# One step table for all engines: two attention layers over four images, with projections placed inside attention and one-tile score banks

## Chip, cores and metric

One core of one Trainium2 chip. The metric is the device time of one execution in microseconds (us); the median of three runs is used. Times within one profiled execution are read from its trace, where the span is the time from the first to the last instruction. Engine names of the profile: PE (TensorE matmuls), PEld (its weight loads), DVE (VectorE), ACT (ScalarE), POOL (GpSimd), SP (SyncE).

## The reference

x is (4, 256, 64, 64) in float32, that is four images of 256 channels by 4096 positions.

```python
# layer 0, per image; x is 256 x 4096
q, k, v = Wq @ x + bq, Wk @ x + bk, Wv @ x + bv      # 32, 32, 256 channels
attn = softmax(q.T @ k, over the rows i)             # 4096 x 4096
x = gamma * (v @ attn) + x
# layer 1, per image
theta = theta_w @ x + theta_b                        # 32 channels, 4096 positions
phi   = maxpool2(phi_w @ x + phi_b)                  # 32 channels, 1024 positions
g     = maxpool2(g_w @ x + g_b)                      # 128 channels, 1024 positions
out   = g @ softmax(theta.T @ phi).T                 # 128 x 4096
x = gamma * (out_w @ out + out_b) + x
```

## The kernel before

**Tiles.** Positions whose attention is computed come in 8 chunks of 512 (`NCH`, `CH`). The keys come in tiles of 128: 32 tiles in layer 0, 8 in layer 1 (`KT`). Scores of a tile are 128 keys x 512 positions. Values and keys are kept in two parts, a high part in fp32r and a low part, the difference; probabilities are split in the same way. So each tile costs one scores matmul, and for each of the 2 (layer 0) or 1 (layer 1) blocks of 128 output channels three matmuls: high by high, high by low (L927, `prob_h`), low by high (L927, `prob_l`).

**Stages.** For each image in turn: `project0` for 8 chunks (keys, queries and values of layer 0, from x rounded by ScalarE, L446, and its rest made by GpSimd, L373), attention of layer 0, `project1` for 8 chunks (g with a max pool, keys and queries of layer 1), prologue maxima, attention of layer 1. x of an image lies whole in SBUF in `x_sb` and is rewritten in place by layer 0 and by layer 1; it is stored and the next image's chunk is loaded into its place by SyncE (L334, L326).

**Softmax.** The greatest score of a position is needed ahead of its chunk. Matmuls `ST` (L832) make the scores transposed, 128 positions x 512 keys, into an auxiliary bank, and VectorE reduces each to a maximum (L605). From the maxima of a chunk VectorE makes `nm_wide` (`finish_max`, L611 to L616), four matmuls `M` (L840) turn it into rows which VectorE writes into `queries` (L623), and the scores matmul then subtracts the maximum by itself. ST and M of chunk n + 1 (layer 0) or n + 2 (layer 1) run within chunk n.

**Step of attention.** A step holds two tiles. TensorE makes the scores of the next step (L914, into one of two `s_ps` of two banks each), then the low matmuls of the last step, then the high ones of this step; the places of ST, M, D1, D2 and Z between them are written out in `PLANS`. ScalarE takes exp twice over 128 x 1024 (L487 into `prob`, L491 into `prob_h`). GpSimd subtracts (L382, `prob_l`). VectorE adds both tiles of `prob` into the PSUM bank `acc` (L704).

**End of a chunk.** ScalarE copies `o_ps[0]` (L502) and `acc` (L509), VectorE copies `o_ps[1]` (L749). D1 (L946) sums over partitions, VectorE takes the reciprocal (L715), D2 (L951) spreads it, VectorE multiplies (L723 in layer 0, L720 in layer 1). In layer 0 VectorE also adds the bias and x (L732). In layer 1 Z (L956) is the output convolution, ScalarE drains it (L517), GpSimd adds x (L389). The fp32 matmuls D1, D2 and Z are two instructions each.

**Order.** Each engine works through its own queue in order; semaphores alone tie the queues together. PSUM has 8 banks: four for `s_ps`, two for `o_ps`, `acc` and `aux`. In the projection stages the four banks of `s_ps` hold the projections, so scores cannot run then.

## Time and profile before

| what | value |
|---|---|
| median of 3 runs | 2927.06 us (2925.76 to 2927.38) |
| the profiled execution | 2925.82 us, of which 2924.0 us span |
| mean granted TensorE clock | 0.97 of full |
| PE busy | 2771.6 us (95%), 12260 matmuls |
| PEld busy | 2156.4 us (74%) |
| DVE busy | 2119.7 us (72%), 3369 instructions |
| ACT busy | 1585.5 us (54%), 1827 instructions |
| POOL busy | 1763.6 us (60%), 776 instructions |
| DMA | 36.41 MB, mean 12 GB/s |

Matmuls are pipelined: the duration of one in the profile, about 0.4 us for 512 columns, is about twice the distance between the starts of two in a row. So TensorE's busy share says only that something was in its pipeline; for the work one counts matmuls and takes the distance of starts.

### The profile page before, as it was taken

How to read it: one execution, taken by the hardware profiler on the slowest of the kernel's cores; microseconds unless marked ns; L12 is line 12 of the kernel's file. 1: busy time of each engine (PE TensorE's matmuls, PEld its weight loads, DVE VectorE, ACT ScalarE, POOL GpSimd, SP SyncE). 2: the span in 40 equal slices, each digit the busy share in tenths (PEclk: the TensorE clock that was granted, in tenths of full speed). 3: DMA queues.
4: the chain of work that ended last, by engine and by line, in shares of the span. 5: the costliest groups of instructions: out<-in, count | busy, mean ns of one | idle time of the engine just before them, and what ended most of it. 6: DMA issues, size and time to landing. Idle time of an engine off the chain costs nothing.

```text
span 2924.0 us, 33409 instructions
## 1 busy us (share of the span) xinstructions
PE 2771.6 (95%) x12260; PEld 2156.4 (74%) x12260; DVE 2119.7 (72%) x3369; ACT 1585.5 (54%) x1827; POOL 1763.6 (60%) x776
## 2 busy tenths in 40 slices
PE   7999999989999999998999999998899999999888
PEld 6877777756787777865677777776567777778665
DVE  7777777676777777767677777776757777777685
ACT  5545545657555555565665555556566545555655
POOL 3665665658466666665746666666574566666557
PEclk9999999989899999998989999999899999999988
DMA  2000000002000000000200000000020000000001
GB/s 68 1 0 1 1 1 1 1 15 72 30 1 1 1 1 1 1 0 22 73 22 1 1 1 1 1 1 1 27 73 17 1 1 1 1 1 1 1 15 44
DMA packets 18131, 36.41 MB, mean 12 GB/s; under 512 B 1200, under 2 KB 1328, under 8 KB 17968
## 3 DMA queue, kind: packets, MB, share of 16 engines
q1 hardware_dynamic: 17408, 33.56, 3.5%
q8 instruction: 97, 1.59, 0.2%
q10 hardware_dynamic: 560, 0.73, 0.1%
q14 instruction: 66, 0.54, 0.1%
HBM read 17.50 MB, written 16.78 MB: 12 GB/s over the span
## 4 chain that ended last, share of the span: by engine, by line
PE 80%; DVE 13%; ACT 3%; issue 3%; DMA 0%; POOL 0%; ACTq 0%; POOLq 0%
PE o_ps L927 52%; PE s_ps L914 9%; PE aux L832 9%; DVE mx L605 5%; PE aux L951 2%; DVE vl L628 2%; DVE acc L704 2%; ACT queries L457 1%; DVE queries L629 1%; PE o_ps L946 1%; PE aux L956 1%; PE aux L840 1%; PE o_ps L956 1%; PE o_ps L832 1%; PE aux L946 1%
## 5 line engine op out<-in xcount | busy, mean ns | idle before, releaser
L382 POOL TENSOR_TENSOR prob_l<-prob,prob_h 128x1024 fp32r<-128x1024 f32 x640 | 1530.5, 2392 | 985.0 <-ACT prob_h L491 983.1
L487 ACT ACTIVATE prob<-s_ps 128x1024 f32<-128x1024 f32 x640 | 657.5, 1027 | 1101.8 <-PE s_ps L914 1078.0
L605 DVE TENSOR_REDUCE mx<-aux 128x1 f32<-128x512 f32 x1088 | 750.6, 690 | 382.5 <-PE aux L832 358.3
L927 PE MATMUL o_ps<-prob_h,vh 128*128 128x512 f32 x2304 | 938.2, 407 | 10.3 <-ACT prob_h L491 3.4
L927 PE MATMUL o_ps<-prob_h,vl 128*128 128x512 f32 x2304 | 913.4, 396 | 0.0
L704 DVE TENSOR_TENSOR acc<-prob,acc 128x512 f32<-128x512 f32 x1216 | 836.5, 688 | 73.4 <-ACT prob L487 60.3
L927 PE MATMUL o_ps<-prob_l,vh 128*128 128x512 f32 x2304 | 685.2, 397 | 1.5 <-POOL prob_l L382 1.5
L491 ACT ACTIVATE prob_h<-s_ps 128x1024 fp32r<-128x1024 f32 x640 | 654.2, 1022 | 0.0
L927 PEld LDWEIGHTS o_ps<-prob_h,vh 128*128 128x128 f32 x2304 | 438.7, 190 | 127.1 <-ACT osb L502 25.0
L927 PEld LDWEIGHTS o_ps<-prob_l,vh 128*128 128x128 f32 x2304 | 435.7, 190 | 102.6 <-POOL prob_l L382 6.0
L927 PEld LDWEIGHTS o_ps<-prob_h,vl 128*128 128x128 f32 x2304 | 438.8, 190 | 94.3 <-issue 6.7
L832 PE MATMUL aux<-keys,queries 96*128 96x512 f32 x1088 | 458.3, 421 | 41.7 <-DVE mx L605 36.3
L914 PE MATMUL s_ps<-queries,keys 128*128 128x512 f32 x1280 | 413.4, 405 | 3.3 <-issue 3.3
L832 PEld LDWEIGHTS aux<-keys,queries 96*128 96x128 f32 x1088 | 208.4, 192 | 138.2 <-DVE mx L605 63.0
L914 PEld LDWEIGHTS s_ps<-queries,keys 128*128 128x128 f32 x1280 | 242.6, 194 | 61.2 <-DVE queries L623 6.7
L373 POOL TENSOR_TENSOR xl<-x_sb,xh 128x1024 fp32r<-128x1024 f32 x64 | 152.3, 2381 | 147.4 <-ACT xh L446 147.4
L605 DVE TENSOR_REDUCE mx<-o_ps 128x1 f32<-128x512 f32 x192 | 131.3, 684 | 6.4 <-PE o_ps L832 4.8
L832 PE MATMUL o_ps<-keys,queries 96*128 96x512 f32 x192 | 90.0, 469 | 16.9 <-DVE mx L605 14.8
L389 POOL TENSOR_TENSOR x_sb<-zc,x_sb 128x512 f32<-128x512 f32 x64 | 81.2, 1273 | 24.1 <-ACT zc L517 24.1
L732 DVE SCALAR_TENSOR_TENSOR x_sb<-osb,gbv,x_sb 128x512 f32<-128x512 f32 x64 | 89.8, 1408 | 0.1
L457 ACT ACTIVATE queries<-s_ps,cols 32x512 fp32r<-32x512 f32 x128 | 87.0, 679 | 3.2
L502 ACT ACTIVATE osb<-o_ps 128x512 f32<-128x512 f32 x64 | 38.2, 597 | 92.2 <-PE o_ps L927 92.2
(72 smaller groups left out, 1822.5 us busy)
## 6 DMA issues: line engine op xcount, KB each, us to landing
x_sb<-x SPq DMA_DIRECT2D x32, 512.0 KB, 3.7
y<-x_sb SPq DMA_DIRECT2D x32, 512.0 KB, 2.8
prob<-w_in ACTq DMA_DIRECT2D x1, 576.0 KB, 5.2
wo<-w_out ACTq DMA_DIRECT2D x1, 128.0 KB, 6.0
cols<-columns ACTq DMA_DIRECT2D x1, 4.5 KB, 6.1
```

Source lines behind the costliest of these rows:

```text
L373: nc.gpsimd.tensor_tensor(out=xl[par][:, :, :], in0=x_sb[:, :, chunk(c)], in1=xh[par][:, :, :].bitcast(f32), op=ALU.subtract).then_inc(xl_ ...
L382: nc.gpsimd.tensor_tensor(out=prob_l[i][:, :, :], in0=prob[i], in1=prob_h[i][:, :, :].bitcast(f32), op=ALU.subtract).then_inc(pl_ready, 1)
L389: nc.gpsimd.tensor_tensor(out=x_sb[:, ct, chunk(n - 1)], in0=zc[:, ct, :], in1=x_sb[:, ct, chunk(n - 1)], op=ALU.add).then_inc(y_ready, 1)
L457: nc.scalar.activation(dst, src, ACT.Identity, bias=cols[rows, COL_KQ[l]:COL_KQ[l] + 1]).then_inc(hi_ready, 1)
L487: nc.scalar.activation(prob[i], s_ps[i][:, :, :], ACT.Exp).then_inc(p_ready, 1)
L491: nc.scalar.activation(prob_h[i][:, :, :], s_ps[i][:, :, :], ACT.Exp).then_inc(ph_ready, 1)
L605: nc.vector.tensor_reduce(out=mx[:, sub, c], in_=aux_bank[bank][:, :], axis=AX.X, op=ALU.max).then_inc(aux_free[bank] if done is None else ...
L704: nc.vector.tensor_tensor(out=acc[:, :], in0=prob[i][:, t, :], in1=acc[:, :], op=ALU.add).then_inc(acc_done, 1)
L732: ins = nc.vector.scalar_tensor_tensor(out=x_sb[:, ct, chunk(n - 1)], in0=osb[:, ct, :], scalar=gbv[:, ct:ct + 1], in1=x_sb[:, ct, chunk(n ...
L832: mm(aux_bank[bank][:, :], queries[0:R3, ds(n * CH + sub * P, P)], keys[0:R3, chunk(c)], start=True, stop=True).then_inc(aux_full[bank], 1)
L914: last = mm(s_ps[i][:, t, :], keys[:, kt * P:(kt + 1) * P], queries[:, chunk(n)], start=True, stop=True)
L927: ins = mm(o_ps[ct][:, :], value, (prob_l if low else prob_h)[s % 2][:, t, :], start=not low and k % 2 == 0 and kt == 0, stop=low and kt = ...
```

## The change

All work is laid out once, in `make_plan`, as jobs at steps of one table of 1280 tiles (32 or 8 per chunk). Every engine walks the same table and takes of each job what is its own part. A tile is one step; scores have three banks of one tile (`SRING`), probabilities four slots of one tile (`RING`), scores are made two tiles ahead (`AHEAD`), splits and sums one. The three banks for jobs are X0, X1 and Y, which is `o_ps[1]` and free in layer 1 only.

Within layer 0's attention of chunk n run the jobs for chunk n - 1 of layer 1: XB (ScalarE adds the bias to x), N (GpSimd adds x), X (rounding and rest), G1, K1, K1K, K1L, T1, T1L (projection of layer 1, VectorE's and ScalarE's parts of it). Within layer 1's attention run the projections K0, V0 (drained by ScalarE, low parts K0L, V0L by VectorE) of chunks 4 to 7 of the next image in chunks 1 to 4, and the maxima of its chunk 0. Between layer 0 and layer 1 of an image stands one list (`before[tile_no(1, b, 0)]`), with the last projection of layer 1 and the first four of the next image; layer 1's scores start behind it (`gated`). Layer 0 of the second to fourth image has no such list. The first image has a list of its own (`before[0]`).

x no longer stays in SBUF. `xp` has two slots for projections of layer 0, the first two loads issued by SyncE and the others by ScalarE. `xa` has four slots: SyncE loads a chunk of x again for layer 0's residual, stores the result to a DRAM tensor `spill`, loads it back for layer 1's residual and stores y. The final part of layer 0's residual moves from VectorE (L732) to ScalarE (bias) and GpSimd (add).

The diff, cut to its core:

```diff
-DIST = (1, 2)
-        x_sb = sb("x_sb", [P, CT, N])
-        s_ps = [pb(f"s_ps{i}", [P, 2, CH]) for i in range(2)]
-        aux_bank = (aux, o_ps[1])
...
+RING = 4
+SRING = 3
+AHEAD = 2
+QSLOTS = 12
+ASLOTS, PSLOTS = 4, 2
+X0, X1, Y = range(3)
...
+def gated(l, b):
+    return l == 1 or b == 0
+def begin_step(h, ahead):
+    l, b, _, _ = tile_at(h)
+    return max(h - ahead, tile_no(l, b, 0) if gated(l, b) else 0)
+def begun_at(g, ahead):
+    return [h for h in range(g, min(g + ahead + 1, TILES)) if begin_step(h, ahead) == g]
...
+    def project0(b, c, banks):
+        k, v0, v1 = banks
+        return [on(Job("K0", 0, b, c, 0), k), on(Job("V0", 0, b, c, 0), v0), on(Job("V0", 0, b, c, 1), v1)]
+    def put(g, place, job):
+        during.setdefault(g, []).append(Entry(place, job))
...
+    lists = []
+    for c in range(NCH):
+        k, v0, v1 = project0(0, c, (X1, Y, X0 if c == 0 else Y))
+        if c == 0:
+            lists += [first[0], first[1], k, Job("K0L", 0, 0, 0, 0), v0, Job("V0L", 0, 0, 0, 0),
+                      v1, Job("V0L", 0, 0, 0, 1)]
+        else:
+            if c + 1 < NCH:
+                lists.append(first[c + 1])
+            st = [maxima(0, 0, 0, c - 1, s, X0) for s in range(SUBS)]
+            lists += [st[0], k, st[1], v0, Job("K0L", 0, 0, c, 0), st[2], Job("V0L", 0, 0, c, 0), v1, st[3],
+                      Job("V0L", 0, 0, c, 1)]
+    lists += [maxima(0, 0, 0, NCH - 1, s, X0 if s % 2 == 0 else X1) for s in range(SUBS)]
+    lists.append(on(Job("M", 0, 0, 0, 0), X0))
+    before[0] = lists
...
+            if prev is not None:
+                put(g, 1, on(Job("D1", *prev, 0), X1))
+                put(g + 2, 1, on(Job("D2", *prev, 0), X1))
+                if prev[0] == 0:
+                    c = prev[2]
+                    put(g + 1, 1, Job("XB", *prev, 0))
+                    put(g + 3, 1, Job("N", *prev, 0))
+                    put(g + 7, 1, Job("X", 1, b, c, 0))
+                    put(g + 10, 1, on(Job("G1", 1, b, c, 0), X1))
+                    put(g + 13, 1, on(Job("K1", 1, b, c, 0), X1))
+                    put(g + 14, 1, Job("K1K", 1, b, c, 0))
+                    put(g + 15, 1, Job("K1L", 1, b, c, 0))
+                    put(g + 17, 1, on(Job("T1", 1, b, c, 0), X1))
+                    put(g + 18, 1, Job("T1L", 1, b, c, 0))
+                else:
+                    for k in range(CT):
+                        put(g + 4 + 2 * k, 1, on(Job("Z", *prev, k), X1))
+                        put(g + 5 + 2 * k, 1, Job("ZA", *prev, k))
+            if n + 1 < NCH:
...
+                steps = [(i, X0) for i in range(27)] + [(i, X1) for i in range(20, 25)]
+                steps.sort()
+                for i, (t, at) in enumerate(steps):
+                    put(g + t, 1 if at == X1 else 3, maxima(0, b, n + 1, i // SUBS, i % SUBS, at))
+                put(g + 28, 1, on(Job("M", 0, b, n + 1, 0), X1))
+            else:
+                for i in range(SUBS * (NCH - 1)):
+                    put(g + i, 3, maxima(1, b, i // SUBS, 0, i % SUBS, X0))
+                if more:
+                    put(g + 21, 1, Job("X", 0, b + 1, 0, 0))
+                    put(g + 27, 1, Job("X", 0, b + 1, 1, 0))
...
+            before[tile_no(1, b, 0)] = (
+                chain1 + [k0] + chain2[:2] + [low("K0L", 0, 0), v00, low("V0L", 0, 0), v01, low("V0L", 0, 1)]
+                + chain2[2:] + [k1_, low("K0L", 1, 0), v10, low("V0L", 1, 0), v11, low("V0L", 1, 1),
+                                Job("X", 0, b + 1, 2, 0)]
+                + chain3 + [Job("X", 0, b + 1, 3, 0)]
+                + [st[0][0], k2, st[0][1], low("K0L", 2, 0), st[0][2], v20, st[0][3], low("V0L", 2, 0), v21, m0,
+                   low("V0L", 2, 1)]
+                + [k3, st[1][0], v30, low("K0L", 3, 0), st[1][1], low("V0L", 3, 0), v31, st[1][2], low("V0L", 3, 1), st[1][3],
+                   Job("X", 0, b + 1, 4, 0)])
...
+            if more:
+                for s, (t, at) in enumerate(((0, X1), (0, Y), (2, Y), (3, Y)) if n < NCH - 1 else
+                                            ((0, X1), (0, Y), (1, X1), (1, Y))):
+                    put(g + t, 3, maxima(0, b + 1, 0, n, s, at))
+                c = n + 3
+                if n >= 1 and c < NCH:
+                    k, v0, v1 = project0(b + 1, c, (X1, X1, X1))
+                    put(g + 1, 1, k)
+                    put(g + 3, 1, Job("K0L", 0, b + 1, c, 0))
+                    put(g + 4, 1, v0)
+                    put(g + 5, 1, Job("V0L", 0, b + 1, c, 0))
+                    put(g + 6, 1, v1)
+                    put(g + 7, 1, Job("V0L", 0, b + 1, c, 1))
+                    if c + 1 < NCH:
+                        put(g + 7, 1, Job("X", 0, b + 1, c + 1, 0))
...
+        xa = [sb(f"xa{i}", [P, CT, CH]) for i in range(ASLOTS)]
+        xp = [sb(f"xp{i}", [P, CT, CH]) for i in range(PSLOTS)]
+        keys = (sb("keys0", [P, KT[0] * P], f32r), sb("keys1", [P, KT[1] * P], f32r))
+        queries = sb("queries", [P, QSLOTS, CH], f32r)
...
+        s_ps = [pb(f"s_ps{i}") for i in range(SRING)]
+        o_ps = [pb(f"o_ps{i}") for i in range(2)]
+        acc = pb("acc")
+        aux = (pb("aux0"), pb("aux1"), o_ps[1])
...
+            for k in range(B * 2 * NCH):
+                l, b, n = k // NCH % 2, k // (2 * NCH), k % NCH
+                store_a(l, b, n)
+                nxt = k + ASLOTS
+                if nxt < B * 2 * NCH:
+                    slot, turn = a_slot(l, b, n)
+                    sp.wait_ge(xa_out[slot], 16 * (turn + 1))
+                    if l == 0:
+                        sp.wait_ge(xl_ready, ROUND[Job("X", 1, b, n, 0)] + 1)
+                    load_a(nxt // NCH % 2, nxt // (2 * NCH), nxt % NCH)
...
+            def entry(job):
+                name, l, b, c, k = job
+                if name == "X":
+                    r = ROUND[job]
+                    src = xa[a_slot(0, b, c)[0]] if l else xp[image0(b, c) % PSLOTS]
+                    pool.wait_ge(xh_ready, r + 1)
+                    nc.gpsimd.tensor_tensor(out=xl[r % 2][:, :, :], in0=src[:, :, :],
+                                            in1=xh[r % 2][:, :, :].bitcast(f32),
+                                            op=ALU.subtract).then_inc(xl_ready, 1)
+                elif name == "N":
+                    slot, _ = a_slot(0, b, c)
+                    pool.wait_ge(xb_ready, CT * image0(b, c) + CT)
+                    for ct in range(CT):
+                        if ct == 0:
+                            pool.wait_ge(normed, image0(b, c) + 1)
+                        else:
+                            wait_free(pool, Job("D2", 0, b, c, 0))
+                        nc.gpsimd.tensor_tensor(out=xa[slot][:, ct, :], in0=osb[:, ct, :], in1=xa[slot][:, ct, :],
+                                                op=ALU.add).then_inc(x1_ready, 1)
...
+            for g in range(TILES):
+                for job in BEFORE.get(g, ()):
+                    entry(job)
+                for h in begun_at(g, 1):
+                    split_prob(h)
+                for e in DURING.get(g, ()):
+                    entry(e.job)
...
+            def exps(h):
+                i, s = h % RING, h % SRING
+                act.wait_ge(s_full, h + 1)
+                wait(act, pl_ready, h - RING + 1)
+                wait(act, acc_done, h - RING + 1)
+                nc.scalar.activation(prob[:, i, :], s_ps[s][:, :], ACT.Exp).then_inc(p_ready, 1)
+                wait(act, av_h, h - RING + 1)
+                nc.scalar.activation(prob_h[:, i, :], s_ps[s][:, :], ACT.Exp).then_inc(ph_ready, 1)
...
+                elif name == "V0":
+                    wait_full(act, job)
+                    at = c * SUBS + 2 * k
+                    nc.scalar.activation(vh[0][:, at:at + 2, :], bank[:, :].rearrange("p (t m) -> p t m", t=2),
+                                         ACT.Copy).then_inc(high_ready, 1)
+                    p = image0(b, c) + PSLOTS
+                    if k == 1 and p < B * NCH:
+                        load_p(p)
...
+            for g in range(TILES):
+                l, b, n, t = tile_at(g)
+                if t == 0 and g:
+                    copy_o(*chunk_before(l, b, n))
+                for job in BEFORE.get(g, ()):
+                    entry(job)
+                for h in begun_at(g, AHEAD):
+                    exps(h)
+                if t == KT[l] - 1:
+                    copy_acc(l, b, n)
+                for e in DURING.get(g, ()):
+                    entry(e.job)
...
+            for g in range(TILES):
+                l, b, n, t = tile_at(g)
+                prev = chunk_before(l, b, n)
+                if t == 0 and prev is not None and prev[0] == 0:
+                    copy_o(*prev[1:])
+                for job in BEFORE.get(g, ()):
+                    entry(job)
+                fresh = t == KT[l] - 1
+                if not fresh:
+                    for h in begun_at(g, 1):
+                        add_prob(h)
+                for e in DURING.get(g, ()):
+                    entry(e.job)
+                if fresh:
+                    for h in begun_at(g, 1):
+                        add_prob(h)
...
+            def scores(h):
+                l, b, n, t = tile_at(h)
+                if t == 0:
+                    wait_free(pe, Job("M", l, b, n, 0))
+                wait(pe, ph_ready, h - SRING + 1)
+                mm(s_ps[h % SRING][:, :], keys[l][:, t * P:(t + 1) * P], queries[:, q_slot(l, b, n), :],
+                   start=True, stop=True).then_inc(s_full, 1)
...
+                if g:
+                    av_low(g - 1)
+                for job in BEFORE.get(g, ()):
+                    entry(job)
+                for h in begun_at(g, AHEAD):
+                    scores(h)
+                entries_at(1)
+                av_high(g, 0)
+                entries_at(2)
+                if VT[l] > 1:
+                    av_high(g, 1)
+                entries_at(3)
```

## Rows read from the trace of the kernel before

**Rows 1.** The page's slices: granted clock in 40 equal parts of the span, tenths of full.
```profile
PEclk9999999989899999998989999999899999999988
```

**Rows 2.** Windows view: stretch, its length, then busy us and instructions (x) by engine, clock, DMA.
```profile
0.00:66.50 66.50, 50.67 (x285) 41.19 (x285) 51.11 (x79) 37.77 (x54) 20.40 (x17) 0.95 0.23 75
...
792.40:1283.00 490.60, 486.16 (x2146) 392.81 (x2147) 356.42 (x549) 254.68 (x270) 306.80 (x129) 0.99 0.00 1
1283.00:1341.80 58.80, 43.66 (x157) 26.68 (x156) 42.56 (x70) 26.54 (x43) 20.75 (x9) 0.84 0.00 0
1341.80:1454.20 112.40, 106.11 (x459) 76.13 (x458) 83.57 (x150) 75.66 (x90) 87.46 (x43) 0.96 0.18 57
1454.20:1519.00 64.80, 56.95 (x309) 43.92 (x307) 45.84 (x72) 38.90 (x56) 25.49 (x14) 0.89 0.10 33
913.30:976.20 62.90, 62.25 (x277) 50.10 (x276) 47.71 (x75) 32.05 (x35) 38.33 (x17) 1.00 0.00 1
1379.40:1394.70 15.30, 14.43 (x66) 10.11 (x65) 12.02 (x23) 10.06 (x12) 12.06 (x7) 1.00 0.22 70
```

**Rows 3.** Timeline at a chunk boundary of layer 0: start, length (us), engine, line.
```profile
1167.63 1.07 PE L927 MATMUL o_ps<-prob_l,vh 128*128 128x512 f32 x4
1168.54 0.61 PE L914 MATMUL s_ps<-queries,keys 128*128 128x512 f32 x2
...
1168.73 0.69 DVE L749 COPY osb<-o_ps 128x512 f32<-128x512 f32 x1 [2.21 <-PE o_ps L927]
...
1169.53 0.47 PE L927 MATMUL o_ps<-prob_h,vh 128*128 128x512 f32 x1
```

**Rows 4.** Timeline of TensorE near the end: a Z and a D2.
```profile
2908.81 1.02 PE L956 MATMUL o_ps<-osb,wo 128*128 128x512 f32 x2
...
2912.72 1.13 PE L951 MATMUL aux<-ident,rsum 128*128 128x128 f32 x8 [0.37 <-DVE rsum L715]
```

**Rows 5.** Windows view within the stage between layers 0 and 1.
```profile
1293.00:1323.00 30.00, 21.50 (x84) 12.45 (x82) 23.38 (x36) 20.46 (x35) 14.19 (x6) 1.00 0.00 1
1323.00:1341.80 18.80, 13.44 (x28) 7.41 (x29) 13.57 (x26) 2.55 (x4) 2.34 (x1) 0.51 0.00 0
```

**Rows 6.** Groups by line and shape: busy us, mean ns, then idle before and releaser.
```profile
L382 POOL TENSOR_TENSOR prob_l<-prob,prob_h 128x1024 fp32r<-128x1024 f32 x640 | 1530.5, 2392 | 985.0 <-ACT prob_h L491 983.1
L605 DVE TENSOR_REDUCE mx<-aux 128x1 f32<-128x512 f32 x1088 | 750.6, 690 | 382.5 <-PE aux L832 358.3
L487 ACT ACTIVATE prob<-s_ps 128x1024 f32<-128x1024 f32 x640 | 657.5, 1027 | 1101.8 <-PE s_ps L914 1078.0 <-DVE acc L704 23.4 <-POOL prob_l L382 0.4
L832 PE MATMUL aux<-keys,queries 96*128 96x512 f32 x1088 | 458.3, 421 | 41.7 <-DVE mx L605 36.3 <-DVE queries L623 4.6
L457 ACT ACTIVATE queries<-s_ps,cols 32x512 fp32r<-32x512 f32 x128 | 87.0, 679 | 3.2
L389 POOL TENSOR_TENSOR x_sb<-zc,x_sb 128x512 f32<-128x512 f32 x64 | 81.2, 1273 | 24.1 <-ACT zc L517 24.1
L502 ACT ACTIVATE osb<-o_ps 128x512 f32<-128x512 f32 x64 | 38.2, 597 | 92.2 <-PE o_ps L927 92.2
```

**Rows 7.** Timeline of DVE and POOL in the projections of layer 1.
```profile
1291.37 0.34 DVE L629 SCALAR_TENSOR_TENSOR keys<-ppool,cols,keys 32x128 fp32r<-32x128 f32 x1 [0.47 <-ACT keys L457]
...
1294.27 2.37 POOL L373 TENSOR_TENSOR xl<-x_sb,xh 128x1024 fp32r<-128x1024 f32 x1 [5.78 <-ACT xh L446]
...
1295.63 1.15 DVE L629 SCALAR_TENSOR_TENSOR keys<-ppool,cols,keys 32x128 fp32r<-32x128 f32 x1 [0.47 <-ACT keys L457]
```

**Rows 8.** The chain that ended last, in order of time, in the first projections.
```profile
18.17 0.92 PE s_ps L848 x4
...
41.52 1.19 DVE mx L605 x2
...
47.03 1.19 DVE mx L605 x2
```

**Rows 9.** The page's DMA issues: KB each, median us from issue to landing.
```profile
x_sb<-x SPq DMA_DIRECT2D x32, 512.0 KB, 3.7
```

1136 lines of the change are left out of this document (461 added, 675 removed), and 4 rows, old and new, of the table PLANS.

## Prediction

> **What bounds the kernel now.** I read the page's slices first, then the busy time by stage, then single steps in order of time. The slices show the granted TensorE clock at 0.8 to 0.9 of full in a few places, which recur with the images [rows 1]. The stage table gives the period of an image (the second): 490.6 us attention of layer 0, 58.8 us of projections of layer 1 and its first maxima, 112.4 us attention of layer 1, 64.8 us of tail, projections of layer 0 and maxima, 726.6 us in all [rows 2]. TensorE is the bound where attention runs: 277 matmuls in the 62.9 us of one chunk of layer 0. Four matmuls of 512 columns start in 0.91 us, 0.228 us each [rows 3]. By the program 256 of them are long (32 scores, 192 for the output, 32 for maxima), 58.4 us, and 20 short (two sums steps, one for M), at 0.11 us each (eight issue within a 1.13 us row whose last 0.25 us is pipeline [rows 4]), 2.2 us. So 60.6 us is work and 2.3 us is stall. In layer 1 a chunk of 15.3 us holds 40 long matmuls (9.1 us), 20 short (2.2) and two output convolutions at 0.85 us each (the row of 1.02 us less its pipeline end [rows 4]): 13.0 us of work, 2.3 of stall [rows 2].
> The two stages between are bound by chains, not by TensorE: 157 and 309 matmuls in 58.8 and 64.8 us, and half the speed (0.51) in the last 19 us of the first [rows 2, 5]. The work of a whole image, counted by the same pitches, is about 650 us. The change goes for the other 75.
>
> **Attention of layer 0.** Work as before, and now the projection of one chunk of layer 1 in each of seven chunks: 12 long matmuls and a transposition, 12 x 0.228 + 0.25 = 3.0 us. It lies on TensorE, so it is paid in full: 63.6 us. Tiles of one bank: a step is 8 matmuls, 1.83 us. ScalarE had two exps of 1024 columns, 1.03 us each; a 512-wide copy is 0.60 [rows 6], so two exps are at most 1.2 and, if they overlap a little, 1.1 us per step: 60%. VectorE has an add and a maximum, 1.2 to 1.4 (0.69 one). GpSimd's difference is 2.39 us at 1024 and an add at 512 is 1.27 [rows 6]: 1.27 of 1.83. None is the bound. Waits per tile instead of per two tiles: 320 more on TensorE in an image. No row shows a wait's own cost. A chunk has some 80 now; its 2.3 us of stall, all put down to them, would be 0.03 each, 10 us an image. I take 0, as the long ones in a row keep 0.228, and leave the 10 us to the range.
> Stalls, by walking the queues from these durations. (a) GpSimd: at step 7 it has the split of x behind its split of tile 8. ScalarE rounds x only behind its exps of tile 9 (scores in at 0.9, 1.1, 1.0), so GpSimd stands until 3.1 us into the step, then works 2.38; the split of tile 9 ends at 6.7 us, and the low matmuls of tile 9 open step 10, at 5.5. Stall 1.2 us, once in a chunk. The two adds of the residual at step 3 (2.5 us, moved here from VectorE) end with 0.2 us to spare. (b) Chunk boundary: before, the high matmul starts 0.99 us after scores behind the last low one [rows 3]. Now the eight sums matmuls lie in front of that wait, which hides ScalarE's copy; but VectorE first adds tile 0 of the next chunk, which waits for the copy of acc, and only then copies o_ps (0.69 us [rows 3]). About 0.5 us of stall. (c) The single bank X0 for maxima: round trip 0.42 + 0.69 us of 1.83 [rows 6], so VectorE may be 0.6 us late; the two normalising multiplications and the low part of the keys go over that by 0.3 us in all. (d) Small gaps left, 1.0 us. Sum 3.0, a chunk 66.6 us. ScalarE's two added bias copies at step 1 find slack. SyncE's queue now writes every chunk of layer 0 out, reads it back and loads x a second time: four transfers where two were. A load lands 3.7 us after issue [rows 9], with three chunks of 15 us or more ahead of its use; cost 0, and 3.7 us a chunk if that lead were gone.
> The first chunk of an image has no projection but the last two convolutions of the image before: 60.6 + 1.7 + 1.7 = 64.0 (60.3 for the first image, which has neither). The last has 28 maxima instead of 32 and no row for M, but two more roundings of x with their stall: 63.6 - 1.4 + 3.0 + 2.4 = 67.6 (65.3 in the last image). Attention is 64.0 + 6 x 66.6 + 67.6 = 531.2 us (527.5 first, 528.9 last), 41 more than before.
> That low part of the keys took 0.34 us while GpSimd stood, and 1.15 us when a GpSimd subtraction of 2.37 us had begun before it, ending with it [rows 7]. It moves from a stage where GpSimd is busy 35% into attention, where it is 61% now and 75% after [rows 2]; between the two durations I take 0.85 us, which (c) contains. The Trainium skill, "SBUF — State Buffer" (section "SBUF: two separate sides"), says that a VectorE operation with two SBUF inputs and a GpSimd operation take one port pair exclusively, the later one waiting for the whole of the other. The rows agree. By it the wait can be all of a 1.27 us split each time, 0.8 more than I take; on the path, 28 x 0.8 = 22 us, 2938 us instead of my sum.
>
> **Between layer 0 and 1.** Layer 1's scores stay behind a gate, with one list ahead of it: the last projection of layer 1, four projections of the next image, eight maxima. Walked from the last low matmul: normalised at 4.9 us, x rounded behind three drains of ScalarE at 9.9, split at 12.4; TensorE meanwhile does three of the projections' halves; layer 1's conv ends at 17.8, VectorE's and ScalarE's drains of it at 21.9; eight maxima (each 1.2 us round trip on one bank), interleaved with two projections, whose drains VectorE takes in between, end at 41. TensorE works 25 of it. The nearest stretches: 84 matmuls in 30 us held the clock at 1.00; 28 in 18.8 us ran at 0.51 [rows 5]. At 0.228 that is 64% and, at most, 34% of the time; mine is 61%, near the first, so I take full clock: 39.5 to 54, taken 41.5 us. In the last image, without the next one's work, the chain alone is 29 us.
>
> **Attention of layer 1.** Chunks 1 to 4 carry a whole projection of the next image: 6 long and 24 half matmuls, 4.3 us. ScalarE then has 16 x 0.5 exps, copies, drains (0.68 for each query part [rows 6]), a rounding and the issue of a load: about 15 us; VectorE 14, GpSimd 15.1 (8 x 1.27 + 2 x 1.27 + 2.38), TensorE 17.3. All four are close, queues are in order and scores are only two tiles ahead: stall 2.5, 19.8 us. The others: 15.1, with 12.8 for the first and 14.1 for the last two. Sum 12.8 + 79.2 + 15.1 + 28.2 = 135.3 us against 112.4. In the last image, with no foreign work and four maxima less a chunk, 109 (11.5 + 5 x 14.2 + 2 x 13.2). There is no gate into the next layer 0: of the 64.8 us nothing stays.
> A period is then 531.2 + 41.5 + 135.3 = 708.0 us, 18.6 less than 726.6.
>
> **The first image** pays. Before, its loads are all in flight early and a chunk costs 5.5 us, VectorE's time (41.52 to 47.03) [rows 8]; its first output matmul starts at 66.5 us [rows 2]. After, only two slots hold x; the load of chunk c + 2 is issued by ScalarE behind its last drain of chunk c, and the rounding of chunk c + 2 is the first thing in ScalarE's list of chunk c + 1. So the list of c + 1 opens with a landing of 3.7 us [rows 9], then rounding 1.05, the three query and key drains 2.0, VectorE's low parts and a maximum and the low value part, together 2.8; and since both value halves use bank Y, the second half's 12 matmuls (1.4 + 0.3) and its drain 0.6 follow. Sum 12.1 us at full clock, 13.5 at half; TensorE is busy 40% there, between the two stretches of [rows 5], so 12.8. The first chunk is done at 18.0, as now, when the second's matmuls start [rows 8]. Six such: 18.0 + 76.8 = 94.8, then the last chunk, four maxima and the first exps, 17.3: first output at 112 us, 45 later. Its cover would be an earlier issue; there is none.
>
> **Sum.** 112 + 527.5 + 41.5 + 135.3 = 816.3; two images of 708.0: 2232.3; the last 528.9 + 29 + 109 + 15 of tail (now the Z at 2908.81 [rows 4] lies 15.2 ahead of the end) = 2914.2 us of span. The profiled run had 1.8 us around its span and lay 1.2 below the median of 2927.06. Forecast 2916.0 us, 0.4% less.
>
> **Rivals.** (1) Faster, 2853: slack absorbs the queue stalls, layer 0 chunks take 65.0 (28 x 1.6) and the twelve loaded chunks of layer 1 18.3 (18 us). For: VectorE loses the residual adds, and a late TensorE gives every other engine time. Against: one bank for maxima, one tile of lead for splits. (2) Slower, 2972: GpSimd's queue in layer 0. The adds at step 3 end with only 0.2 us to spare; if each entry of GpSimd comes some 0.5 to 1 us later, both stall, a chunk takes 68.6, 28 x 2.0 = 56 us. It decides from 0.4 us per chunk on (11 us over 28). For: the walk puts one entry past due. Against: a late TensorE gives the others time back. (3) Slower, 2961: the change doesn't take away what it says. The gate before layer 1 stays, and with gaps in it the clock falls: 54 instead of 41.5 us thrice, and 8 more at the front, 45 us. For: 0.51 in the same place now. Against: more matmuls per us than there.
>
> **Chances.** Forecast (2895 to 2935) 0.40, of which 0.27 lies below, 0.08 within, 0.05 above; rival 1 0.25; rival 2 0.22; rival 3 0.13. A measurement of this kernel can tell about 0.2% (6 us) from no change. Faster 0.27 + 0.25 = 0.52, same 0.08, slower 0.40. The range goes to both sides, 2840 to 2975 us.
>
> **What would show it.** Chunks of layer 0 at 66.6 us with a TensorE wait for the split of tile 9; first output matmul at 112 us; from the last output matmul of layer 0 to the first of layer 1 41 us at clock 1.00; loaded chunks of layer 1 at 20 us; no gap into the next image. It is wrong if the first output comes before 90, or a layer 0 chunk is under 65 or over 68 us.

## The result, and the profile after

The changed kernel takes 2949.15 us (median of six runs, 2935.74 to 2955.05) beside 2927.22 us for the kernel before on the same chip: a ratio of 1.007, 95% interval 1.0047 to 1.0093. It is 0.7% slower; the forecast was 2916.0 us, 0.4% faster. The profiled execution took 2952.56 us, of which 2950.8 us is span, 26.8 us more than before's 2924.0.

The page of the changed kernel: totals, the clock in slices, the two groups that changed most.

```profile
span 2950.8 us, 39091 instructions
...
PE 2757.0 (93%) x12260; PEld 2180.1 (74%) x12260; DVE 2008.1 (68%) x3303; ACT 1750.7 (59%) x3171; POOL 1949.9 (66%) x1480
...
PEclk7799999998999999999899999999999999999989
...
DMA packets 44280, 87.10 MB, mean 30 GB/s; under 512 B 2736, under 2 KB 2864, under 8 KB 44080
...
L427 POOL TENSOR_TENSOR prob_l<-prob,prob_h 128x512 fp32r<-128x512 f32 x1280 | 1639.7, 1289 | 751.6 <-ACT prob_h L490 744.2
L487 ACT ACTIVATE prob<-s_ps 128x512 f32<-128x512 f32 x1280 | 768.5, 600 | 974.2 <-PE s_ps L765 973.5
```

TensorE issues the same 12260 matmuls. Its busy time fell by 15 us and the span rose by 27, so this column does not tell the story. Against [rows 1] the slices changed place: the first two stand at 0.7 (0.9 before), where the first image now spends 50 us more, while the dips between the layers are shallower. In tiles of half the size GpSimd's splits cost 7% more (1530.5 us in [rows 6]) and ScalarE's first exps 17% more (657.5 us there).

The windows view, stretch by stretch, answers to [rows 2]. Columns: stretch, length, busy us (instructions) of PE, PEld, DVE, ACT, POOL, granted clock, DMA share, GB/s.

```profile
0.00:115.70 115.70, 69.60 (x284) 54.62 (x284) 53.12 (x76) 36.64 (x54) 20.16 (x17) 0.75 0.22 70
444.20:510.60 66.40, 64.77 (x290) 52.47 (x290) 47.24 (x78) 39.52 (x73) 45.89 (x36) 1.00 0.05 17
641.20:684.70 43.50, 32.78 (x171) 26.18 (x170) 23.90 (x41) 22.03 (x34) 11.98 (x7) 0.86 0.24 73
684.70:702.30 17.60, 16.58 (x56) 11.52 (x57) 13.89 (x25) 10.95 (x22) 13.17 (x11) 0.78 0.01 1
702.30:722.80 20.50, 18.77 (x96) 13.94 (x95) 15.39 (x28) 14.58 (x26) 11.87 (x10) 1.00 0.14 48
722.80:745.80 23.00, 21.79 (x94) 15.97 (x94) 15.11 (x27) 15.20 (x27) 15.02 (x12) 0.85 0.21 69
745.80:769.10 23.30, 21.66 (x95) 16.03 (x95) 15.16 (x27) 15.26 (x27) 15.10 (x12) 0.85 0.20 68
792.10:807.40 15.30, 14.16 (x66) 10.16 (x65) 12.39 (x23) 10.92 (x21) 11.87 (x10) 1.00 0.16 53
```

These are the time to the first output matmul, one chunk of layer 0, the stage between layers 0 and 1, and chunks 0, 1, 2, 3 and 5 of layer 1 of the first image. Compare the fifth row with the next two: the same jobs in 20.5 us at full clock and in 23.0 and 23.3 at 0.85. By the program the chunks hold the same matmuls.

The ledger of the three images that project a next one, first output matmul to first output matmul. The stage between the layers is counted from the last tile's high matmuls (641.2 in the first image), 0.9 us ahead of the last low one, from which the forecast walked:

| us | forecast | image 1 | image 2 | image 3 |
|---|---|---|---|---|
| to the first output matmul | 112 | 115.7 | | |
| attention of layer 0 | 527.5, 531.2, 531.2 | 525.5 | 527.0 | 527.0 |
| between the layers | 41.5 | 43.5 | 43.8 | 42.2 |
| attention of layer 1 and into the next image | 135.3 | 151.3 | 150.8 | 149.4 |

The last image took 524.0 + 32.4 + 104.0 + 14.2 = 674.6 us, where 681.9 was forecast (528.9 + 29 + 109 + 15). A period is 721.6 us (image 2), 5.0 less than the 726.6 before; 18.6 less was forecast. The first image is 43.6 us later than before at the first output matmul of the second (836.0 against 792.4), image 2 gives back 5.0, the other two 11.8 together: 26.8.

### The profile page after: what moved, and what is told of

The parts are those of the page before. It is cut to its first block, busy times and chain, and to the rows that moved or that the text cites. A ratio compares the mean times of both kernels' runs of the same rounds, so it can differ in the third digit from the quotient of the medians.

```text
span 2950.8 us, 39091 instructions
## 1 busy us (share of the span) xinstructions
PE 2757.0 (93%) x12260; PEld 2180.1 (74%) x12260; DVE 2008.1 (68%) x3303; ACT 1750.7 (59%) x3171; POOL 1949.9 (66%) x1480
## 2 busy tenths in 40 slices
DMA packets 44280, 87.10 MB, mean 30 GB/s; under 512 B 2736, under 2 KB 2864, under 8 KB 44080
## 4 chain that ended last, share of the span: by engine, by line
PE 77%; issue 9%; DVE 5%; ACT 5%; POOL 4%; DMA 1%; POOLq 0%; ACTq 0%; DVEq 0%
PE o_ps L797 30%; PE o_ps L775 16%; PE s_ps L765 8%; PE aux L828 8%; POOL prob_l L427 3%; PE aux L808 3%; PE aux L841 2%; ACT prob_h L490 2%; DVE mx L650 2%; PE aux L837 2%; PE aux L845 1%; PE aux L812 1%; PE aux L862 1%; PE o_ps L828 1%; PE o_ps L862 1%
## 5 line engine op out<-in xcount | busy, mean ns | idle before, releaser
L427 POOL TENSOR_TENSOR prob_l<-prob,prob_h 128x512 fp32r<-128x512 f32 x1280 | 1639.7, 1289 | 751.6 <-ACT prob_h L490 744.2
L487 ACT ACTIVATE prob<-s_ps 128x512 f32<-128x512 f32 x1280 | 768.5, 600 | 974.2 <-PE s_ps L765 973.5
L775 PE MATMUL o_ps<-prob_l,vh 128*128 128x512 f32 x2304 | 756.0, 400 | 37.4 <-POOL prob_l L427 37.0
L490 ACT ACTIVATE prob_h<-s_ps 128x512 fp32r<-128x512 f32 x1280 | 762.1, 595 | 0.0
L765 PE MATMUL s_ps<-queries,keys 128*128 128x512 f32 x1280 | 509.2, 399 | 0.8 <-DVE queries L669 0.8
L436 POOL TENSOR_TENSOR xl<-xp,xh 128x1024 fp32r<-128x1024 f32 x32 | 76.0, 2378 | 167.4 <-ACT xh L529 167.4
L436 POOL TENSOR_TENSOR xl<-xa,xh 128x1024 fp32r<-128x1024 f32 x32 | 76.5, 2391 | 52.2 <-ACT xh L529 52.2
L447 POOL TENSOR_TENSOR xa<-osb,xa 128x512 f32<-128x512 f32 x64 | 82.1, 1305 | 20.2 <-DVE osb L682 20.2
L837 PEld LDWEIGHTS aux<-ones,psums 128*128 128x128 f32 x512 | 62.4, 191 | 44.0 <-issue 43.6
L512 ACT ACTIVATE queries<-aux,cols 32x512 fp32r<-32x512 f32 x116 | 78.9, 680 | 19.0 <-PE aux L812 17.9
```

The costliest lines, as they stand in the source:

```text
L427: nc.gpsimd.tensor_tensor(out=prob_l[:, i, :], in0=prob[:, i, :], in1=prob_h[:, i, :].bitcast(f32), op=ALU.subtract).then_inc(pl_ready, 1)
L436: nc.gpsimd.tensor_tensor(out=xl[r % 2][:, :, :], in0=src[:, :, :], in1=xh[r % 2][:, :, :].bitcast(f32), op=ALU.subtract).then_inc(xl_read ...
L487: nc.scalar.activation(prob[:, i, :], s_ps[s][:, :], ACT.Exp).then_inc(p_ready, 1)
L490: nc.scalar.activation(prob_h[:, i, :], s_ps[s][:, :], ACT.Exp).then_inc(ph_ready, 1)
L765: mm(s_ps[h % SRING][:, :], keys[l][:, t * P:(t + 1) * P], queries[:, q_slot(l, b, n), :], start=True, stop=True).then_inc(s_full, 1)
L775: last = mm(o_ps[ct][:, :], value(vh, l, t, ct), prob_l[:, h % RING, :], start=False, stop=t == KT[l] - 1)
```

## Experiments

Each kernel is the changed kernel with one edit, unless it says otherwise. Ratios are against the kernel before, run beside it; the changed kernel itself stands at 1.007. Four kernels (the fill, the earlier rounding, GpSimd's queue and the first try on the first image) ran on a chip where the kernel before takes 2923.36 us, and the last two beside 2923.15; that is 4 us less than the 2927.22 beside the changed kernel, so a difference of their medians holds 4 us of chip. Chunk times are distances of the first output matmuls of chunks in the profiled execution. Two theories were open for layer 1. A: the loaded chunks (those with a projection of the next image) lose the clock in small stalls, and that is the larger part of the miss. B: their queues alone take 23 us.

**Keep TensorE busy at the boundary.** Five matmuls whose results are overwritten unread, around the sums at the start of chunks 1 to 5 of layer 1 (three images), so at both ends of every loaded chunk:

```
 elif name == "D1":
+    if filled:                      # layer 1, chunks 0 to 4
+        for _ in range(3): mm(dst, wh, wh)
     pe.wait_ge(psums_ready, ...)
     ...                             # the eight sums matmuls
+    if filled:
+        last.then_inc(full[at], 1)
+        wait(pe, free[X1], ...)
+        for _ in range(2): mm(aux[X1], wh, wh)
```

> Only change: at the first step of chunks 1 to 5 of layer 1 (images 1 to 3) TensorE gets five matmuls of 512 columns more, into free banks, three ahead of the sums and two behind them, where it waits in the changed kernel (0.86 us for the copy of acc, 0.56 us for the copy of o_ps). Their results are overwritten, so the output is the same. Theory A (the loaded chunks of layer 1 take 23 instead of 19.8 us because the granted clock falls to half for 6.8 us of each, and it falls because TensorE stands around the chunk boundary): the clock keeps 1.00 in most of them, loaded chunks take 19.8 to 20.5 us, the whole about 2925 us although work was added. Rival B (the queues of the four engines cost the 23 us by themselves, the clock is only a by-product): chunks stay at 23 us or grow by up to 1 us, the whole 2950 to 2965 us.

Measured: 2930.22 us (2925.8 to 2934.93, ten runs), ratio 1.0022 (1.0012 to 1.0032). Windows view of this kernel, chunks 0, 2 and 3 of layer 1:

```profile
682.60:700.30 17.70, 15.86 (x61) 11.49 (x62) 14.37 (x26) 11.40 (x22) 13.87 (x11) 0.90 0.01 3
720.90:741.40 20.50, 19.52 (x101) 14.77 (x100) 15.06 (x27) 15.05 (x27) 14.93 (x12) 1.00 0.22 77
741.40:761.90 20.50, 19.51 (x100) 14.75 (x100) 15.06 (x27) 15.04 (x27) 14.93 (x12) 1.00 0.23 77
```

All twelve loaded chunks take 20.5 us, none at half clock: 22.6 us less than in the changed kernel. Work was added, and the kernel became 19 us faster (15 when each is set against the kernel before beside it). Theory A holds. The timeline of TensorE in the changed kernel shows how the clock is lost:

```profile
743.62 0.40 PE L765 MATMUL s_ps<-queries,keys 128*128 128x512 f32 x1
744.48 1.02 PE L837 MATMUL aux<-ones,psums 128*128 128x1 f32 x8 [0.47 <-ACT psums L509]
745.82 0.50 PE L797 MATMUL o_ps<-prob_h,vh 128*128 128x512 f32 x1 [0.32 <-ACT osb L501]
...
748.17 1.11 PE L833 MATMUL o_ps<-ident_r,nm_wide 128*128 128x128 f32 x4 [0.54 <-DVE mx L650]
749.08 0.68 PE L808 MATMUL aux<-xh,wh 128*96 128x512 f32 x1
749.56 0.63 PE L808 MATMUL aux<-xh,wl 128*96 128x512 f32 x1
749.99 0.63 PE L808 MATMUL aux<-xh,wh 128*96 128x512 f32 x1
```

The starts of single rows, less the 0.23 us that a matmul takes, give the gaps: the sums matmuls start 0.6 us late, behind ScalarE's copy; they are of one column each; and the next output matmul stands another 0.3 behind the profile's end of them. Both waits are gone in the kernel with the fill. The clock is granted at half from 747.2 to 754.0, and matmuls of 512 columns then start 0.43 us apart (749.56, 749.99), where they start 0.23 apart at full clock. 6.8 us at half would be 3.4 us of work lost; such a chunk lost 2.5 to 2.9. The waits do not bring the fall every time: the boundary into the first loaded chunk has the same one before its sums (0.48 us at 701.42), and that chunk keeps full clock.

**Round the next x earlier.** In loaded chunks the rounding of the next chunk of x at step 2 instead of 7, so that ScalarE doesn't stand before the boundary with it.

```
-  put(g + 7, 1, Job("X", 0, b + 1, c + 1, 0))
+  put(g + 2, 1, Job("X", 0, b + 1, c + 1, 0))
```

> Only change: in the loaded chunks of layer 1 the rounding of the next x and its rest (ScalarE 1.06 us, GpSimd 2.38 us) stand at step 2 instead of step 7, so ScalarE's copies at the chunk boundary are not behind the rounding. Theory A (TensorE's wait at the boundary lets the clock fall): the wait of 0.56 us behind the sums goes, 0.6 to 1.0 us a chunk at once, and if the clock then stays up in part of the chunks 2 to 4 us a chunk: whole 2915 to 2940 us. Rival B (queues alone): 11 chunks x 0.6 to 1.0 = 7 to 11 us, the clock unchanged, 2940 to 2945 us. Rival C (GpSimd's queue is the tight one in these chunks; its 2.38 us in step 2 make later splits late): no gain or a loss.

Measured: 2927.5 us (2924.7 to 2931.57), ratio 1.0012 (1.0002 to 1.0021). The loaded chunks stay at 20.5 us (the fourth 20.1), so the 0.6 to 1.0 us that were to come off at once did not; but 11 of 12 are at full clock (one takes 21.9). The whole lies 22 us below the changed kernel (18 against the kernel before beside it) with no work removed; the loaded chunks, 246.2 us instead of 268.6, put that down to the clock again.

**Leave the traffic out.** The spill transfers carry 32 of 512 columns; the rest of layer 1's residual isn't computed from the right x.

```
+  sp.dma_start(xa[slot][:, :, 0:32], source[:, ..., n * CH:n * CH + 32])
+  return
   sp.dma_start(xa[slot][:, :, :], source[:, ..., chunk(n)])
```

> The transfers to and from the spill tensor move 32 of 512 columns, so layer 1's residual is wrong in the rest; number, place and waits of the transfers stay. Rival under test: the added traffic (87 MB against 36) is what the change pays for. If so the whole falls by 20 us or more. Theory: the transfers are hidden by three chunks of lead and cost nothing: every stage keeps its length, loaded chunks 20.5 us where the clock stays and 23 where it falls, whole 2930 to 2955 us.

Measured: 2938.65 us (2936.01 to 2944.18, three runs), ratio 1.0044. Chunks of layer 0 take 66.4 us as before the edit, loaded chunks 20.5, 20.5, 20.5, 20.1 in the first image, 22.1, 23.1, 23.4, 21.6 in the second and 20.5, 20.5, 22.1, 22.6 in the third. The whole is 10 us lower, but its three runs lie within the range of the changed kernel's six, and no chunk at full clock became shorter than in the kernels with the traffic. So the spill's part of the added traffic (36.41 MB before, 87.10 after) costs nothing that shows; the second load of x was left in and is not tested. More telling: within one execution the same instructions take 20.5 us where the clock holds and 23 where it falls.

**Put the projections back into the list.** Chunks 4 to 7 of the next image are projected between the layers instead of within layer 1, the same instructions. The query ring has 12 slots, so these queries overwrite those of the first four chunks of layer 1, whose output is that of other queries.

```
+  for c in range(4, NCH):
+      before[tile_no(1, b, 0)] += [kc, K0L, va, V0L, X(c + 1), vb, V0L]
...
-  if n >= 1 and c < NCH:
+  if n >= 99:
```

> One part undone: chunks 4 to 7 of the next image's layer 0 projections stand at the end of the list between the layers instead of inside layer 1's attention; everything else, the maxima inside it too, as in the changed kernel. By my account a loaded chunk of layer 1 costs 20.5 us at full clock and 23 at half for 6.8 us, an unloaded one 15.2: 4 x (5.3 to 7.8) = 21 to 31 us less an image there. A projection in the list costs a chain of about 7 to 8 us (key and query drains 2.0, low parts 1.5, value parts, rounding 1.06 and rest 2.4): 28 to 32 us more. Theory: about the same whole, 2945 to 2965 us, with clock lost in the list instead. Rival (projections inside attention are the cheap place, TensorE alone pays 4.3 us): 3 x 4 x (7.5 - 4.3) = 38 us more, 2980 us and above.

Measured: 2956.64 us (2952.97 to 2960.98), ratio 1.0103. Windows view of this kernel, the list, and chunk 3 of layer 1:

```profile
639.00:711.20 72.20, 52.97 (x291) 42.81 (x290) 34.52 (x56) 37.71 (x57) 19.60 (x11) 0.91 0.22 67
757.50:775.60 18.10, 16.96 (x65) 12.73 (x66) 12.33 (x23) 10.85 (x21) 12.39 (x11) 0.81 0.17 59
```

The list takes 72.2 us instead of 43.5, 7.2 us for each projection moved there; layer 1 takes 123.5 instead of 151.3, 7.0 less for each. So a projection within layer 1 costs at its own chunk nearly what it costs outside, although TensorE's part of it is 6 long and 24 half matmuls, 4.3 us in the forecast. At full clock it is 5.2 (20.5 against 15.3). Without load a chunk can still lose the clock: 15.3 becomes 18.1 in three of twelve and 16.9 in a fourth.

**GpSimd's queue in layer 0.** The forecast's stall (a). GpSimd's part of X goes one step later, behind its split of tile 9.

```
   put(g + 7, 1, Job("X", 1, b, c, 0))
+  put(g + 8, 1, Job("XL", 1, b, c, 0))
...
+  if name == "X" and l == 1 and c < NCH - 1: return    # GpSimd
+  if name in ("X", "XL"): ...
```

> Only change: GpSimd's part of the rounding of layer 1's x in layer 0's attention stands one step later (step 8) than ScalarE's (step 7), so GpSimd no longer stands waiting for ScalarE ahead of the split of tile 9. Theory (one stall of 1.2 us a chunk at step 10, as forecast): chunks of layer 0 65.2 instead of 66.4 us, the whole 2914 to 2920 us less what the clock scatters (about 10 us). Rival (the stall only moves to the split of tile 10 or to the conv at step 10): chunks 66.0 to 66.4 us, whole unchanged.

Measured: 2900.72 us (2896.38 to 2908.48), ratio 0.9924 (0.9905 to 0.9943): faster than both kernels. Chunks of layer 0 take 65.1 us instead of 66.4, every one. The changed kernel's timeline of POOL at that place, then its waits over five chunks (total, times, longest), then the same view of this kernel over five chunks:

```profile
980.13 1.29 POOL L427 TENSOR_TENSOR prob_l<-prob,prob_h 128x512 fp32r<-128x512 f32 x1 [0.36 <-ACT prob_h L490]
982.92 2.39 POOL L436 TENSOR_TENSOR xl<-xa,xh 128x1024 fp32r<-128x1024 f32 x1 [1.50 <-ACT xh L529]
985.27 5.01 POOL L427 TENSOR_TENSOR prob_l<-prob,prob_h 128x512 fp32r<-128x512 f32 x4
```

```profile
PEld o_ps L775 <- POOL prob_l L427: 7.1, 5, 1.4
PEld o_ps L797 <- issue: 3.0, 6, 0.5
PEld aux L837 <- issue: 2.8, 5, 0.6
PEld aux L828 <- DVE mx L650: 1.1, 5, 0.2
```

```profile
PEld aux L840 <- issue: 2.8, 5, 0.6
PEld o_ps L800 <- issue: 2.5, 5, 0.5
PEld aux L831 <- DVE mx L653: 1.1, 5, 0.2
```

GpSimd stands 1.50 us for the rounding with a free engine, then four splits run back to back, late. 1.4 us of TensorE's wait per chunk becomes none, and nothing else grows. 28 chunks by 1.3 us are 36 of the 48 us gained (45 against the kernel before beside it); the rest lies in layer 1, whose loaded chunks kept the clock more often in this execution too (253.5 us instead of 268.6), and in the first image (112.0 instead of 115.7).

**The first image, three tries.** First, the rounding of chunk c + 1 behind the first value half of chunk c, ahead of the second:

```
-  lists.append(first[c + 1])         # rounding, first in the list of chunk c
   lists += [st[0], k, st[1], v0, K0L, st[2], V0L]
+  lists.append(first[c + 1])
   lists += [v1, st[3], V0L]
```

> Only change: in the first image's list the rounding of chunk c + 1 stands behind the drain of the first value half of chunk c, not ahead of the whole list, so the load's landing (3.7 us) is hidden by ScalarE's drains. Theory (the first image's 49 us delay is the chain landing, rounding, drains, second value half): the cycle falls from 12.8 to about 8 us, the first output matmul comes at 85 to 92 us instead of 115.7, the whole 2920 to 2928 us. Rival (the shared bank Y for both value halves and the single bank X0 for maxima bind): cycle 11 to 12 us, the whole above 2940 us.

Measured: first output matmul at 109.9 us, the whole at 2937.02 us (2932.5 to 2937.91), ratio 1.0042. The expectation fell; the rival's condition fits, though its 2940 us were not reached. Kernels whose first image was not edited have it at 111.0 to 115.7, so 1 to 6 us of this are the edit's. The order alone does not free the chain.

Second, the load of chunk c + 2 behind the drains of keys and queries instead of behind the last value drain:

```
 ACT, K0:  biased(... queries ...)
+          load_p(image0(b, c) + PSLOTS)
 ACT, V0:
-          if k == 1: load_p(image0(b, c) + PSLOTS)
```

> Only change: ScalarE issues the load of chunk c + 2 behind its key and query drains of chunk c (the slot is free by then), not behind the last value drain; the order of all jobs stays as in the changed kernel. Theory (the first image pays for the landing of 3.7 us in every chunk, in series with drains and the value halves on one bank): cycle 12.8 minus 3.7 minus what the half clock adds, 8.5 to 9.5 us, first output matmul at 90 to 95 us instead of 115.7, whole 2925 to 2932 us with the changed kernel's scatter of clock. Rival (the three banks bind, as in the run where the rounding was moved and the cycle stayed at 11 to 13 us): first output after 105 us.

Measured: first output at 109.3 us, the whole at 2946.33 us (2936.61 to 2950.47), ratio 1.0061. ScalarE stands before every rounding for the landing in the changed kernel (its timeline; the transfer issued at 31.22 is rounded at 34.93):

```profile
31.22 0.60 ACT L549 ACTIVATE vh<-o_ps 128x512 fp32r<-128x512 f32 x1 [5.38 <-PE o_ps L865]
31.22 0.39 ACTq L478 DMA_DIRECT2D xp<-x  x1
34.93 1.06 ACT L529 ACTIVATE xh<-xp 128x1024 fp32r<-128x1024 f32 x1 [3.12 <-DMA xp<-x]
...
38.16 0.60 ACT L549 ACTIVATE vh<-o_ps 128x512 fp32r<-128x512 f32 x1 [0.21 <-PE o_ps L865]
43.95 0.60 ACT L549 ACTIVATE vh<-o_ps 128x512 fp32r<-128x512 f32 x1 [5.19 <-PE o_ps L865]
```

but taking that wait away gave 2 to 6 us: the roundings come 11.2 instead of 12.8 us apart. The 5.38 and 5.19 us before the second value half were the next thing late. TensorE's timeline of the changed kernel shows what it waits for:

```profile
40.99 0.58 PE L862 MATMUL o_ps<-wh,xh 128*128 128x256 f32 x1 [2.63 <-DVE vl L628]
...
45.05 0.50 PE L828 MATMUL aux<-keys,queries 96*128 96x512 f32 x1 [0.78 <-DVE mx L650]
```

The second value half waits for bank Y, until VectorE has read the first half's low part out of it, and a maximum waits for the last one to leave X0.

Third, everything at once. The two edits above that worked (XL, X early), the early load, the three score banks S0 to S2 also as job banks in the two lists that run while no scores are needed, two banks for maxima there instead of one, and in layer 1 M and the low keys at step 2:

```
-X0, X1, Y = range(3)
+X0, X1, Y, S0, S1, S2 = range(6)
...
-    k, v0, v1 = project0(0, c, (X1, Y, X0 if c == 0 else Y))
+    k, v0, v1 = project0(0, c, (S0 if c % 2 == 0 else S1, S2, Y))
...
-    k0, v00, v01 = project0(b + 1, 0, (X1, Y, X1))
+    k0, v00, v01 = project0(b + 1, 0, (S0, S1, S2))
...
-    put(g + 1, 1, on(Job("M", 1, b, n + 1, 0), Y))
+    put(g + 2, 1, on(Job("M", 1, b, n + 1, 0), Y))
```

> All repairs together: GpSimd's part of the rounding a step later in layer 0 (-1.3 us in 28 chunks, 36 us); early issue of the loads and, in both gated lists, the three score banks as further places for projections and two banks for maxima (first output at 70 to 80 us instead of 115, list between the layers 33 to 38 instead of 43.5 us three times); in layer 1 the rounding at step 2, the rows of M and the low keys one step later and earlier, away from waits of 0.8 and 0.5 us (20.5 to 19.2 us a loaded chunk). Sum from 2950: 36 + 40 + 24 + 16, and 20 to 25 us if the clock keeps full in layer 1: 2810 to 2840 us. If the list between the layers is bound by its chain and not by banks it keeps 40 us and the whole is some 15 us higher.

Measured: 2824.06 us (2819.97 to 2825.38, four runs), ratio 0.9647 (0.9632 to 0.9661), 3.5% faster than the kernel before. Windows view: first image, the stage between, one loaded chunk.

```profile
0.00:68.40 68.40, 51.96 (x284) 40.87 (x284) 51.80 (x76) 36.83 (x54) 20.30 (x17) 0.95 0.37 119
585.30:620.10 34.80, 28.95 (x172) 24.00 (x170) 21.98 (x37) 22.07 (x34) 11.51 (x7) 0.95 0.30 92
657.30:678.10 20.80, 18.84 (x97) 13.96 (x96) 15.04 (x27) 15.27 (x27) 14.94 (x11) 1.00 0.24 78
```

The same 284 matmuls reach the first output matmul in 68.4 us instead of 115.7, at clock 0.95 instead of 0.75. The stage between takes 34.8, 34.5 and 36.9 us instead of 43.5, 43.8 and 42.2. The loaded chunks do not reach the expected 19.2: ten take 20.7 to 20.8 us at full clock and two 22.3. VectorE, now with its low parts at step 2, is late with queries and maxima (0.59 and 0.84 us of TensorE's waiting, up to 684.74 and 687.00). That part of the expectation fell.

Two more kernels take the 47.3 us of the first image apart. The first is the last kernel with the load late again:

```
-  load_p(...) behind the drains of keys and queries
+  load_p(...) behind the last value drain
```

> The kernel of e8 with one thing put back: the load of x for chunk c + 2 of the first image is issued again behind the last value drain of chunk c, not behind its query and key drains. In e8 a chunk of the first projections takes 5.7 us (ScalarE's roundings at 30.01, 35.69, 41.39), the load goes out 1.0 us behind a rounding, lands 3.7 later, 1.0 us ahead of the next rounding. Theory A (the landing is a second bound that the banks had covered): the load goes out with the last drain, directly ahead of the rounding that wants it, so every chunk waits for 3.7 us of landing: 9.4 us a chunk, six or seven times 3.7 = 22 to 26 us, first output matmul at 91 to 94 us instead of 68.4, the whole at 2846 to 2852. Theory B (only banks and order bound the first projections, as the run with the early load alone suggested): first output at 68 to 72, the whole at 2824 to 2828.

Measured: one run, 2826.74 us; first output matmul at 74.9 us. ScalarE's timeline of this kernel:

```profile
31.56 0.37 ACTq L477 DMA_DIRECT2D xp<-x  x1
35.37 1.06 ACT L528 ACTIVATE xh<-xp 128x1024 fp32r<-128x1024 f32 x1 [3.22 <-DMA xp<-x]
...
37.26 0.38 ACTq L477 DMA_DIRECT2D xp<-x  x1
...
38.41 0.60 ACT L548 ACTIVATE vh<-s_ps 128x512 fp32r<-128x512 f32 x1
38.91 0.59 ACT L548 ACTIVATE vh<-o_ps 128x512 fp32r<-128x512 f32 x1
41.05 1.06 ACT L528 ACTIVATE xh<-xp 128x1024 fp32r<-128x1024 f32 x1 [1.55 <-DMA xp<-x]
...
48.85 1.06 ACT L528 ACTIVATE xh<-xp 128x1024 fp32r<-128x1024 f32 x1 [3.06 <-DMA xp<-x]
```

The landing does bind here, 6.5 us in all: neither the 22 us of theory A nor nothing. The whole says the same: this kernel is 96.4 us faster than the one before beside it, the last one was 102.9. Chunks alternate 5.7 and 7.8 us: where both value halves are ready, the load goes out at 37.26, ahead of the two drains that precede it in the queue (38.41, 38.91), 1.65 us ahead of the second. The second kernel also has the old order of the first list:

```
-  lists += [k] + st[:1] + [v0] + st[1:2] + [K0L] + st[2:3] + [v1, V0L] + st[3:] + [V0L]
+  lists += st[:1] + [k] + st[1:2] + [v0, K0L] + st[2:3] + [V0L, v1] + st[3:] + [V0L]
```

> The kernel of e9 with a second thing put back, in the first projections alone: the order of the list as the changed kernel has it (a maximum first, then query and key convolution, maximum, first value half, low part of the keys, maximum, low value part, second value half, maximum, low part); the three score banks and the two banks for maxima stay, and the late load. If the banks alone free the first projections (theory A), this costs at most 1 us a chunk over e9: first output within 7 us of it. If the order was the larger part (theory B), a chunk goes back toward the 12.8 us of the changed kernel: first output at 105 us or more. Together with e9 the two split the 47 us between first output at 115.7 and 68.4 into landing, order and banks.

Measured: one run, 2838.79 us; first output matmul at 80.8 us, 5.9 later. So of 47.3 us the landing is 6.5, the order 5.9, and the banks with the clock that they keep 34.9 (the clock up to the first output matmul is 0.91 here, 0.75 in the changed kernel). These are single profiled executions, and 115.7 is the greatest of the six with an unedited first image; from the least, 111.0, the banks' share is 30. So it is 30 to 35 us, and the two small shares are rough. The score banks and the second bank for maxima were not tried one without the other. Alone, order and early load had each given 6 us at most: behind a third thing that is late they show little.

## Why the prediction was wrong, point by point

**Attention of layer 0: right, and its stall was real.** 66.4 us a chunk against 66.6. Stall (a) was put at 1.2 us; the trace shows 1.4 of waiting and its removal gives 1.3. What is left at the chunk boundary, two waits of 0.5 and 0.6, answers to (b) and part of (d). Waits for maxima, stall (c), are 0.2 a chunk against 0.3. The tight entry of rival 2, the residual adds at step 3, never held TensorE up; the 68.6 us of rival 2 did not come. Only the last chunk was too dear, by 2.5 us (67.6 forecast; 64.2, or 65.1 up to the last low matmul, measured), and the first image's first chunk too cheap by the same (60.3 against 62.9).

**The low keys.** I charged 0.85 us each, between the two durations of [rows 7]. All 32 took 0.34:

```profile
L629 DVE SCALAR_TENSOR_TENSOR keys<-ppool,cols,keys x32: 342/343/344, 212.0 to 2815.6; 32x128 fp32r<-32x128 f32 x32
```

(changed kernel, durations in ns, least, median, greatest.) Each fell between two operations of GpSimd, which is busy 69% of a chunk (45.89 of 66.40 us); 28 of them started within 0.012 us of the end of a split, always 0.03 us behind VectorE's own last operation. The rule of the Trainium skill, "SBUF — State Buffer" (section "SBUF: two separate sides"), was not tested by that, since nothing overlapped. Its 2938 us came nearer to the measured time than my sum, but for a reason that was not at work.

**The first image: right in time, not in its cause.** 115.7 us against 112, a cycle of 12.8 as worked out (31.22, 43.95, 56.77 above). (The terms that I named for the cycle add up to 11.9 us, not 12.1.) I wrote that its cover would be an earlier issue. The early load alone gave 2 to 6 us. The banks gave 30 to 35: Y for both value halves and X0 for all maxima were in my sum as ordinary terms, where they were what the rest waited for.

**Between the layers.** 43.5, 43.8 and 42.2 us against 41.5, inside the range I gave, and 0.9 less each when counted from the last low matmul, as I had walked. The clock was 0.86, 0.91 and 0.95 with the same instructions, not 1.00. Rival 3 had this mechanism, the clock, at this place. The last image's stage took 32.4 us against 29 at clock 0.69; how much of the 3 us is the clock no run shows.

**Attention of layer 1: the step that failed.** The forecast says "stall 2.5, 19.8 us" for a loaded chunk and 12.8 for the first. The ledger: twelve loaded chunks took 268.6 us against 237.6, three first chunks 51.9 against 38.4, the other nine together 1.0 more: 45.5 us, more than the whole miss of 36.6; all other terms together gave 8.9 back. Of the 31.0 us in loaded chunks, 8.4 are stalls that were sized too small (12 by 0.7: 20.5 us at full clock instead of 19.8, stall 3.2 instead of 2.5) and 22.6 are the clock, which I had weighed between the layers and at the front only and taken as full wherever attention runs. Before, layer 1 stood at 0.96 [rows 2] with one chunk of it at 1.00; that 0.96 over 112.4 us was a sign that attention of layer 1 loses the clock somewhere, and it was passed over. Cut finer, the trace of before has the loss at the two ends (the first 12.40 us at 0.92, the last 24.20 at 0.86) and none in the five chunks between:

```profile
1354.20:1430.00 75.80, 71.58 (x321) 50.34 (x321) 60.03 (x110) 49.56 (x60) 59.06 (x30) 1.00 0.18 56
1430.00:1454.20 24.20, 23.12 (x95) 17.65 (x96) 12.49 (x20) 17.79 (x22) 19.85 (x11) 0.86 0.27 88
```

So it showed that this attention can lose the clock, not yet that the loaded chunks would. The first chunks, 17.1 to 17.6, take 15.4 to 15.7 in most executions that keep the clock there: about 2 us are clock, and the other 2.8 I put down to a start with only two tiles of scores ahead, which no run tests. Nor does a run take the 0.7 us of stall apart. Rival 3 was the right mechanism at the wrong place. That its 45 us equal the 45.5 of layer 1 is luck: the clock has about 28 of these (22.6 and three times 2), stalls and starts the rest.

A slip of the sum is small beside that: the profiled run lay 1.2 us below its median, which I named and did not add; the sum gives 2917.2, not 2916.0.

What the chances missed is that the four engines of a loaded chunk were close to each other (14 to 17 us of work each). I took this to cost only the stall. A chunk like that also has gaps wherever one queue is late, here at a boundary whose matmuls are short.

## What to carry to other kernels

Price a stall on TensorE twice: its length, and the work behind it at half the clock, as it happened here in 10 of 12 chunks whose gap lay beside short matmuls. A stage's mean clock a little under 1 says that this happens there already; cut the stage by chunks to see where. And where two projections share one bank, try the idle banks before the order of the list or the loads: here an edit to what was not late next showed little, alone.
